# A router's weights spread over the partitions: through DRAM scratch, or through TensorE

## What is computed

```python
# attention: 16 heads of 16, causal and linear
q, k, v = split(xn @ wqkv); q, k = relu(q), relu(k)
y = einsum(q, cumsum(k v^T)) / (einsum(q, cumsum(k)) + 1e-5);  y @ wo
# ffn: 8 experts, two chosen for a token, four of them MLPs
scores = sigmoid(xn @ Wr)
idx = top_k(scores + router_bias, 2)
w = scores[idx] / (sum(scores[idx]) + 1e-9);  cw[token, idx] = w
hid_e = silu(xn @ Wg_e) * (xn @ Wu_e);  routed = sum_e cw[:, e] * (hid_e @ Wd_e)      # e = 0..3
routed += cw[:, 4] * xn + cw[:, 6] * xn + cw[:, 7] * relu(xn)
ffn = routed + causal depthwise conv of 4 taps over xn + conv_b
```

## Time and profile before

| | |
|---|---|
| runs, median of three | 1793.89 us |
| span of the profiled execution | 1787.3 us |
| TensorE matmul busy | 1698.4 us (95%), 14688 instructions |
| TensorE weight load busy | 1362.2 us (76%) |
| VectorE busy | 1485.0 us (83%) |
| ScalarE / GpSimd busy | 776.7 us (43%) / 787.5 us (44%) |
| DMA | 39.03 MB, 22 GB/s on average |
| mean granted TensorE clock | 0.988 |

### The profile page before, as it was taken

How to read it: one execution, slowest core, us unless ns; L and a number is a source line. 1 busy time by engine, 2 the same in 40 slices (tenths; PEclk the granted TensorE clock), 3 DMA queues, 4 the chain that set the end, 5 groups by cost and what they waited for, 6 DMA issues and landing times.

```text
span 1787.3 us, 38335 instructions
## 1 busy us (share of the span) xinstructions
PE 1698.4 (95%) x14688; PEld 1362.2 (76%) x14688; DVE 1485.0 (83%) x3052; ACT 776.7 (43%) x1617; POOL 787.5 (44%) x869
## 2 busy tenths in 40 slices
PE   5999999999999999999999999999999999999998
PEld 4877778777787777787777877778876788777787
DVE  7888878888788888888888888788887888888886
ACT  5435444344443445343544434444344444344442
POOL 2544425454244533454433445334553345444353
PEclk9999999999999999999999999999999999999999
DMA  2000000000000000000000000000000000000000
GB/s 88 25 2 25 24 26 25 13 14 25 25 25 13 13 25 26 24 25 1 25 26 25 25 16 10 25 25 25 25 1 25 25 25 25 1 25 24 25 13 13
DMA packets 38043, 39.03 MB, mean 22 GB/s; under 512 B 1880, under 2 KB 37592, under 8 KB 37856
## 3 DMA queue, kind: packets, MB, share of 16 engines
q1 hardware_dynamic: 37856, 36.43, 6.2%
HBM read 19.65 MB, written 16.78 MB: 20 GB/s over the span
## 4 chain that ended last, share of the span: by engine, by line
PE 71%; DVE 16%; issue 8%; ACT 4%; POOL 0%; DMA 0%; DVEq 0%; POOLq 0%
PE ring L299 32%; PE scores L339 12%; PE num L380 6%; PE state_add L393 3%; DVE ql L766 3%; PE num L371 3%; PE ring L413 3%; DVE ksum L759 3%; PE turned L406 3%; PE ring L353 2%; PE ring L290 2%; DVE sm L777 2%; PE ring L481 2%; PE state_add L353 2%; DVE wsum L727 1%
## 5 line engine op out<-in xcount | busy, mean ns | idle before, releaser
L777 DVE TENSOR_TENSOR sm<-scores,tables_s 128x512 f32<-128x512 f32 x512 | 327.0, 680 | 114.4 <-PE scores L339 103.9
L648 POOL TENSOR_TENSOR hl<-hid,hh 128x512 fp32r<-128x512 f32 x128 | 163.5, 1277 | 484.6 <-ACT hh L502 484.6
L624 POOL TENSOR_TENSOR kl<-kT,kh 128x512 fp32r<-128x512 f32 x64 | 83.1, 1300 | 346.1 <-ACT kh L502 342.8
L339 PE MATMUL scores<-ql,kh 32*128 32x256 f32 x1024 | 173.3, 331 | 58.5 <-DVE ql L766 40.2
L502 ACT ACTIVATE ktok<-turned 128x256 f32<-128x256 f32 x128 | 49.0, 383 | 413.4 <-PE turned L406 413.4
L790 DVE RECIPROCAL rden<-den 128x256 f32<-128x256 f32 x128 | 223.3, 1745 | 3.1 <-ACT den L566 0.7
L339 PEld LDWEIGHTS scores<-ql,kh 32*128 32x128 f32 x1024 | 98.4, 185 | 157.2 <-issue 108.5
L299 PE MATMUL ring<-xl,wgu_h 128*128 128x512 f32 x448 | 195.6, 437 | 0.0
L299 PE MATMUL ring<-xh,wgu_l 128*128 128x512 f32 x448 | 180.3, 403 | 0.0
L299 PE MATMUL ring<-xh,wgu_h 128*128 128x512 f32 x448 | 179.3, 400 | 0.0
L502 ACT ACTIVATE vp<-ring 128x256 f32<-128x256 f32 x96 | 35.7, 388 | 305.0 <-PE ring L299 305.0
(11 more groups left out here) (148 smaller groups left out, 4746.9 us busy)
## 6 DMA issues: line engine op xcount, KB each, us to landing
x_t<-in_L_attn_x_dram SPq DMA_DIRECT2D x32, 512.0 KB, 3.5
out_dram<-x_t SPq DMA_DIRECT2D x32, 512.0 KB, 2.9
hid<-in_L_attn_wqkv_dram SPq DMA_DIRECT2D x2, 384.0 KB, 4.6
sm<-in_L_ffn_Wg_dram SPq DMA_DIRECT2D x2, 256.0 KB
sm<-in_L_ffn_Wu_dram SPq DMA_DIRECT2D x2, 256.0 KB
yT<-in_L_ffn_Wd_dram SPq DMA_DIRECT2D x1, 512.0 KB, 5.0
ksum<-in_L_attn_wo_dram SPq DMA_DIRECT2D x1, 256.0 KB, 5.3
tables_s<-in_tables_dram SPq DMA_DIRECT2D x1, 209.0 KB, 3.6
```

What stands on the lines that cost most here:

```text
L339: ins = mm(SB[f % 2][:, g * 2 * P:(g + 1) * 2 * P], k[rows, g, ts], q[rows, g, :, ts], start=n == 0, stop=n == 2)
L624: pool.tensor_tensor(kl[:, g, :], kT[:, g, :], kh[:, g, :].bitcast(F32), ALU.subtract).then_inc(s_kl, 1)
L648: pool.tensor_tensor(hl[:, t, :], hid[:, t, :], hh[:, t, :].bitcast(F32), ALU.subtract).then_inc(s_hl, 1)
L777: dve.tensor_tensor(heads.rearrange("p g (a n) -> p g a n", a=2), SB[f % 2][:, :].rearrange("p (g a n) -> p g a n", g=C, a=2), causal_s[:, ...
```

## The change

The router's weights go from `cw` to a scratch tensor in DRAM, `cw_rows` (expert, tile, token), by four DMAs of 128 x 4 single float32 numbers, and come back with one DMA that reads the scratch's 2048 numbers once for each of the 128 partitions into `cwb` (128 x 2048 float32, 8 KB a partition, 1 MB in all). Both are issued by SyncE in the batch, ahead of the store; it waits for `s_cw` first, and for the scatters' completion (`cw_out`) between the two. VectorE waits for the load (`cw_in`) once a batch, ahead of `hid` of tile 0, and reads `cwb` there in place of the bank. `cws`, `cwT`, `sel`, their instructions and semaphores go. TensorE's waits that stood at them now name what last used the bank (`s_sig`).

```diff
+    cw_rows = nc.dram_tensor("cw_rows", (E, T, P), F32, kind="Internal").ap()
-        sel = sb("sel", [2 * E, E, P], F32R)
-        cws = sb("cws", [P, T, 2 * E], F32R)
-        cwT = sb("cwT", [2 * E, BT], F32R)
+        cwb = sb("cwb", [P, E, BT])
@@ sync, setup and batch
-            sp.dma_start(st_sel, expert_rows).then_inc(expert_in, 16)
+                sp.wait_ge(s_cw, at(s, j, 1, 1))
+                with nc.allow_non_contiguous_dma(reason="the router's weights are turned"):
+                    for t in range(T):
+                        sp.dma_start(cw_rows[:, t, :].rearrange("e p -> p e"), cw[:, t, 0:E]).then_inc(cw_out, 16)
+                sp.wait_ge(cw_out, at(s, j, 16 * T, 16 * T))
+                sp.dma_start(cwb[:, :, :].rearrange("p e n -> p (e n)"),
+                             cw_rows.rearrange("e t n -> (e t n)").partition_broadcast(P)).then_inc(cw_in, 16)
@@ tensor, small(t)
-                        pe.wait_ge(s_cwT, at(s, j, 1, 1))
+                        pe.wait_ge(s_sig, at(s, j, T, T))
-                    if t == 0:
-                        pe.wait_ge(s_sig, at(s, j, T, 3))
-                    else:
-                        pe.wait_ge(s_hid, at(s, j, T, t))
-                    mm(R[2][:, :], sel[:, t, :], cwT[:, :], start=True, stop=True).then_inc(s_cwp, 1)
@@ tensor, batch
-                pe.wait_ge(s_cws, at(s, j, 1, 1))
-                for t in range(T):
-                    ins = nc.tensor.transpose(TR[0:2 * E, t * P:(t + 1) * P], cws[:, t, :].bitcast(F32), ident_s[:, :])
-                ins.then_inc(s_cwtr, 1)
@@ tensor, output, t == 0
-                        pe.wait_ge(s_hid, at(s, j, T, T))
+                        pe.wait_ge(s_sig, at(s, j, T, 3))
@@ scalar
-                        act.wait_ge(s_cwtr, at(s, j, 1, 1))
-                        copy(cwT[:, :], TR[0:2 * E, :]).then_inc(s_cwT, 1)
-            copy(sel[:, :, :], st_sel).then_inc(set_up, 1)
@@ vector
-                own(dve.tensor_copy(cws[:, :, 0:E], cw[:, :, 0:E]), s, j)
-                dve.tensor_tensor(cws[:, :, E:2 * E], cw[:, :, 0:E], cws[:, :, 0:E].bitcast(F32),
-                                  ALU.subtract).then_inc(s_cws, 1)
-                    dve.wait_ge(s_cwp, at(s, j, T, t + 1))
-                    dve.tensor_tensor(hid[:, t, :], R[2][:, :], gu[:, :], ALU.mult).then_inc(s_hid, 1)
+                    if t == 0:
+                        dve.wait_ge(cw_in, at(s, j, 16, 16))
+                    dve.tensor_tensor(hid[:, t, :], cwb[:, t, :], gu[:, :], ALU.mult).then_inc(s_hid, 1)
```

More of the change, by code:

```diff
@@ L128, in layer_kernel @@
         st_r = ksum[:, 0, 1, 0:C * NR].rearrange("p (c n) -> p c n", c=C)
-        st_sel = ksum[0:2 * E, 1, 0, 0:E * P].rearrange("p (e n) -> p e n", e=E)
         R = [bank(f"ring{k}") for k in range(3)]
@@ L172, in layer_kernel @@
         s_cw = sem("s_cw")
-        s_cws = sem("s_cws")
-        s_cwtr = sem("s_cwtr")
-        s_cwT = sem("s_cwT")
+        cw_out = sem("cw_out")
+        cw_in = sem("cw_in")
         s_qks = sem("s_qks")
@@ L183, in layer_kernel @@
         s_gu = sem("s_gu")
-        s_cwp = sem("s_cwp")
         s_hid = sem("s_hid")
@@ L227, in layer_kernel @@
         EARLY = len(SPLITS)
-        SPLITS += [(expert_in, 5, wgu_h[:, 0], wgu_l[:, 0], st_g), (expert_in, 5, wgu_h[:, 1], wgu_l[:, 1], st_u)]
+        SPLITS += [(expert_in, 4, wgu_h[:, 0], wgu_l[:, 0], st_g), (expert_in, 4, wgu_h[:, 1], wgu_l[:, 1], st_u)]
         SPLITS += [(out_in, 2, wd_h[:, :, :], wd_l[:, :, :], st_d), (out_in, 2, wo_h[:, :, :], wo_l[:, :, :], st_o)]
@@ L232, in layer_kernel @@
         OWN_SETUP = 1 + (TAPS - 1)
-        OWN_BATCH = 1 + 11 + 1 + (TAPS - 1)
+        OWN_BATCH = 1 + 10 + 1 + (TAPS - 1)
         def settled(engine):
@@ L407, in small @@
                     ins.then_inc(s_ktr, 1)
-                    if t == 0:
-                        pe.wait_ge(s_sig, at(s, j, T, 3))
-                    else:
-                        pe.wait_ge(s_hid, at(s, j, T, t))
-                    mm(R[2][:, :], sel[:, t, :], cwT[:, :], start=True, stop=True).then_inc(s_cwp, 1)
                 pe.wait_ge(w_split, N_SPLITS)
-                pe.wait_ge(set_up, 4)
+                pe.wait_ge(set_up, 3)
                 pe.wait_ge(s_sig, at(s, j, T, 1))
@@ L854, in _ @@
             dve.wait_ge(tables_in, 16)
-            dve.wait_ge(set_up, 4)
+            dve.wait_ge(set_up, 3)
             for tap in range(TAPS):
```

## The result

The changed kernel takes 1998.1 us (median of four runs, 1990.9 to 2008.8); the kernel before took 1795.6 us in the same comparison. The ratio on record is 1.116, 95% interval 1.110 to 1.122: 11.6% slower, where I had forecast 3% faster and a range up to 1880 us. Further down, two executions in the slow state are left out of the times: one of 1949 us of four of the kernel "changed, filled", and one of 8956 us of the kernel before beside it.

What follows compares the result with a forecast made beforehand. TensorE was taken as the bound, 71% of the chain, DMA 0%. From 1793.9 us, 55.7 us of removed work went and 4 us for slow landings came: 1742 us, own range 1730 to 1762, reaching up to 1880.

Steps and rivals of the forecast that it cites:

- What goes, and what the path keeps: TensorE's 8-row products and VectorE's cast and subtraction go; tile 0 keeps 0.45 us, tiles 1 to 3 0.43 each: 1.74 us a batch.
- my upper end: Gain per batch if VectorE never becomes the path: 0.30 + 4 x 0.43 = 2.02 us, 65 us in all.
- The scatters' landing, 2.9 us after the last issue: SyncE's last scatter was taken to land as the store does, 2.9 us after issue, at 807.4 us.
- My upper bound: Scatters' latest landing: 47 ns a piece for all 128 pieces of an engine, 803.05 + 1.4 + 6.0 = 810.5 us.
- my lower bound of 13: Scatters' earliest landing: 13 ns a piece, from small packets of loads, 1.8 us after the last issue, at 806.3 us.
- The broadcast, 5.0 us: The 1 MB load into `cwb` lands 5.0 us after issue, at 812.5 us, 1.3 us ahead of `hid`.
- Their removal only lengthens that wait: nothing: Four transposes of `cws` end before TensorE's 1.14 us wait for `ql`; removing them gains nothing.
- `hid` beside GpSimd: In tiles 1 to 3 `hid` may wait 0.74 us for GpSimd, inside 1.33 us of cover: nothing; uncovered 2.2 us a batch.
- Late landing: Rival: `cwb` lands late for tile 0's `hid`; a batch changes by L - 1.74 us; L = 3.2, 1841 us; chance 0.44, slower 0.29.
- TensorE's wait before the third scores group: Sign in tile 0: the wait for VectorE's masks near 0.7 us; above 2.4 us the change is slower.

Runs made afterwards that it cites:

- changed, filled: The changed kernel, its DMAs kept, plus unread TensorE work: eight transposes, a product in tile 0 and 20 products before the long wait; 1921.9 us, ratio 1.078.
- the pair without a transfer: The changed kernel without scatters and broadcast, `cwb` loaded once in setup with other numbers: 1767.6 us; the same plus unread TensorE work: 1708.6 us.
- the removed work with TensorE filled: The changed kernel without scatters and broadcast, `cwb` loaded once, plus eight unread transposes and one unread product on TensorE; 1708.6 us, ratio 0.955.

## Why the prediction was wrong

- *What goes, and what the path keeps* (1.74 us a batch): right in kind, a little small. At the same clock the batches follow each other at 52.0 us (54.0 before), 2.0 us less, my upper end (0.30 + 4 x 0.43), so that tile 0 seems to keep its product's 0.43 us as well.
- *The scatters' landing, 2.9 us after the last issue*: the step that failed. It is 10.0 us, and `cwb` lands 16.3 us after `s_cw` (11.5 + 4.8) where 10.8 were free. My upper bound failed as well, because it priced pieces by the time that they hold a DMA engine (47 ns at most), and the price was not there: a packet took 7.6 ns, under even my lower bound of 13, and the engines were through in 3 us. The packets' durations in a trace could not have told it. No row of before showed several small writes into neighbouring bytes, and I should have kept that end open and not closed it with a row on another resource.
- *The broadcast, 5.0 us*: right, 4.8. Whatever 16 engines lose on reading the same 8 KB, the sum held without it.
- *Their removal only lengthens that wait: nothing* (the four transposes): the second failed step. At the same clock it is nothing, but the clock falls: 2.8% on the kernel before, and 59 us in the pair without a transfer, where the second wait, in place of the 8-row product, has its part. I had read the fall of the clock after an idle stretch and used it only for the late-landing rival.
- *`hid` beside GpSimd*: right. It takes up to 1.22 us beside GpSimd (0.82 us on average after, 0.68 before), and that is covered.
- *Late landing*, the rival, was the case in its place and its rule, not in its mechanism, which was again the time of a DMA engine. TensorE's wait before the third scores group, 2.4 us or more of which would mean slower, is 6.63. All lateness is passed on: in the filled kernel VectorE waits 5.9 us a batch (190.1 us in 32), and the batch at full clock is 5.8 us longer than without a transfer. The rival took L = 3.2 us; with L = 5.5 (16.3 - 10.8) its formula gives 1793.9 + 32 x 3.76 = 1914 us. The rest up to 1998 is the clock, to which the rival gave no price.

The loss in its parts, as the recorded ratios to before: the removed work with TensorE filled, 0.955; the lateness on top of it, 1.078 / 0.955 = 1.128 (some 213 us; VectorE's waits for `cwb` in that run sum to 190.1 us); the clock on top of that, 1.116 / 1.078 = 1.036 (76 us). The first two steps are not free of the clock: it goes from 0.988 to 0.996 in the first and back to 0.988 in the second, so about 1% of each is the clock's. How the clock's loss divides between the long wait and the two short ones is not separated.

## What to carry to other kernels

When data is turned in memory, do not write single numbers side by side: copy the numbers of a partition together first, so that a piece fills its own 64 bytes (0.17 us on VectorE against 10 us of landing here), and take the landing, not the packets, as the price. Before work is taken off TensorE beside a wait, look at what it is doing in the microseconds around that wait: work that is on nobody's path may be what keeps it at 2.4 GHz, and unread work in its place can be worth more than the removal. Compare such versions at the same granted clock, batch by batch if need be, or the change in the clock is taken for the change in the work.

## What the runs showed of the hardware

- 2048 writes of 4 bytes, 16 into each 64 bytes of DRAM: completion 10.0 us after the last issue; 2048 writes, each into its own 64 bytes: 2.9 us; 128 pieces of 64 bytes: 1.42 us from issue to the next DMA's issue. The Trainium skill, "DMA: Bandwidth & Descriptors" (section Anatomy of one DMA), gives a DMA about 2 us of fixed cost, for transfers issued from GpSimd; this one, issued by SyncE, was under it.
- A broadcast of 8 KB of DRAM to 128 partitions lands in 4.8 us (4.5 to 6.7).
- VectorE's product of two SBUF operands of 128x512 takes 0.68 us without a step, 1.03 us when one is read with a step of 64 bytes, 1.07 us at 16 bytes.
- In the kernel before, four small transposes a batch taken out of a wait of TensorE (with ScalarE's copy of them) bring the granted clock of the whole execution from 0.988 to 0.950; the wait grows from 1.26 to 1.68 us on average. Four more change nothing (0.990).
